# Destination stage: the first layer's two products over the mean's 48 rows stand first, one on partitions 0 to 47 and one on partitions 64 to 111

## The reference

```
x = layernorm(x + L0(x))    # [X, AX, AAX, AAAX] @ W + b, A = the weighted edges
x = layernorm(x + L1(x))    # the edge-attribute MLP, below
x = layernorm(x + L2(x))    # two-head attention over the edges
x = layernorm(x + L3(x))    # (x + 3*A'x) / 4
```

```
feat = concatenate([x, out1, out2, out3, u[batch]], axis=1)   # 128 + 48 (sum) + 48 (max) + 48 (mean) + 16
h = relu(feat @ W1 + b1)                                      # W1 has 256 columns
out = h @ W2 + b2;  return out + x
```

## Time and profile before

| | |
|---|---|
| Time, median of 3 runs | 6439.19 us (6438.15 to 6440.65) |
| Profiled execution, span | 6434.0 us |
| Instructions in the span | 102247 |
| PE busy | 4506.4 us (70%) |
| DVE busy | 4375.3 us (68%) |
| POOL busy | 4350.5 us (68%) |
| ACT busy | 3113.9 us (48%) |

### The profile page before, as it was taken

One profiled execution on the slowest core, in us unless ns is written; L12 is line 12 of the kernel. 1 busy time (PEld: TensorE's weight loads), 2 busy tenths in 40 slices (PEclk: granted clock), 3 DMA queues, 4 the chain that ended last, 5 costly groups with the idle time before them and its releaser, 6 DMA issues. The chain is left out here.

```text
span 6434.0 us, 102247 instructions
## 1 busy us (share of the span) xinstructions
PE 4506.4 (70%) x25328; PEld 3190.2 (50%) x25328; DVE 4375.3 (68%) x8181; ACT 3113.9 (48%) x6470; POOL 4350.5 (68%) x4335
## 2 busy tenths in 40 slices
PE   0059479999888799999989999978788784432200
PEld 0047367877666577777754444444444442221100
DVE  7866368888788688888853333349999996753310
ACT  0047368887666455555533333338888884110000
POOL 0057777774777577777746666647777776777777
PEclk9999789999999899999999999998888886555555
DMA  0023257777898799999955555543444435963311
GB/s 24 4 72 110 60 180 242 243 241 219 259 287 285 205 263 262 262 263 261 261 166 165 163 163 164 166 130 113 116 115 116 115 115 177 323 198 94 96 44 40
DMA packets 896637, 1090.56 MB, mean 169 GB/s; under 512 B 137109, under 2 KB 543521, under 8 KB 895492
## 3 DMA queue, kind: packets, MB, share of 16 engines
q1 hardware_dynamic: 757158, 816.08, 41.7%
q0 software_dynamic: 137984, 221.55, 13.3%
q10 hardware_dynamic: 1344, 51.38, 2.0%
HBM read 652.84 MB, written 497.99 MB: 179 GB/s over the span
## 5 line engine op out<-in xcount | busy, mean ns | idle before, releaser
L978 PE MATMUL bank<-ident,gat 128*128 128x128 f32 x2352 | 430.4, 312 | 641.8 <-DVE zT L1934 555.5
L1088 PE MATMUL bank<-W2s,hT 128*128 128x128 f32 x6272 | 779.5, 278 | 78.4 <-ACT hT L1343 78.4
L1073 PE MATMUL bank<-x1T,W1x 128*128 128x512 f32 x1568 | 776.5, 608 | 35.8 <-ACT x1T L1262 33.1
L1088 PEld LDWEIGHTS bank<-W2s,hT 128*128 128x128 f32 x6272 | 736.5, 193 | 104.9 <-ACT hT L1343 102.9
L753 POOL DMA_INDIRECT pays<-PAY,s_q x392 | 378.1, 965 | 487.9 <-DVE s_v L1800 340.0
L978 PEld LDWEIGHTS bank<-ident,gat 128*128 128x128 f32 x2352 | 297.2, 161 | 792.7 <-issue 577.0
L1272 ACT ACTIVATE mbuf<-t 128x512 f32<-128x512 f32 x490 | 310.1, 633 | 716.9 <-DVE t L1968 443.7
L978 PE MATMUL bank<-ident,x 128*128 128x128 f32 x3136 | 487.5, 279 | 195.9 <-DVE x L1901 176.7
L1343 ACT ACTIVATE hT<-bank,b1u 128x512 f32<-128x512 f32 x784 | 491.4, 677 | 248.7 <-PE bank L1076 236.3
L727 POOL DMA_INDIRECT gat<-X,d_x x392 | 392.8, 1002 | 293.9 <-issue 233.3
L1913 DVE TENSOR_TENSOR gat<-gat,pays 128x512 f32<-128x512 f32 x392 | 270.3, 689 | 451.8 <-DMA gat<-X,pays 369.0
(11 more groups left out here) (367 smaller groups left out, 11522.7 us busy)
## 6 DMA issues: line engine op xcount, KB each, us to landing
X<-x SPq DMA_DIRECT2D x588, 256.0 KB, 2.6
fB<-row_s_same SPq DMA_DIRECT2D x392, 256.0 KB
Y<-x SPq DMA_DIRECT2D x294, 256.0 KB, 3.6
xT<-in_x_fm SPq DMA_DIRECT2D x196, 256.0 KB
ffB<-rows_last_notlast SPq DMA_DIRECT2D x98, 512.0 KB
out_rows<-Y ACTq DMA_DIRECT2D x28, 1792.0 KB, 9.9
Z1T<-zT SPq DMA_DIRECT2D x98, 256.0 KB
Z1E<-zE SPq DMA_DIRECT2D x98, 256.0 KB
```

The source lines that it names most:

```text
L978: mm = pe.transpose(dst[:, t, :], tiles[t], ident[:, :])
L1073: mm = pe.matmul(bH[h][:, :, :], W1x[:, cols], x1T[s][:, :], start=True, stop=kind != "d")
L1088: mm = pe.matmul(bMLP[:, t, :], hT[h][s][:, t * P:(t + 1) * P], W2s[:, h, :], start=False, stop=h == HC - 1, skip_group_check=True)
```

## The change

In the destination stage the two W1m products stand ahead of the others. The product for the second half of the columns takes its weights and its data from partitions 64 to 111 in place of 0 to 47; for this the rows of W1 and the mean are loaded on these partitions too. The other four products follow, W1a and then W1x for each half. In other stages `chain_b2` is as it was (one W1x product for each half).

```
             for t, a in ((W1a[0:AF, :], W1[P:P + AF, :]),
                          (W1a[AM:AK, :], W1[P + AF:P + 2 * AF, :]),
-                         (W1m[0:AF, :], W1[P + 2 * AF:P + 3 * AF, :])):
+                         (W1m[0:AF, :], W1[P + 2 * AF:P + 3 * AF, :]),
+                         (W1m[AM:AK, :], W1[P + 2 * AF:P + 3 * AF, :])):
...
             def att_load(i, s):
-                if void(sp, i, s, ("ld_att", i, 32), ("ld_last", i, 16)):
+                if void(sp, i, s, ("ld_att", i, 48), ("ld_last", i, 16)):
...
-                sp.dma_start(mnt[s][0:AF, :], MNT[:, epos(g)]).then_inc(S("ld_att", s), 16)
+                for first in (0, AM):
+                    sp.dma_start(mnt[s][first:first + AF, :], MNT[:, epos(g)]).then_inc(S("ld_att", s), 16)
...
-            pe.wait_ge(S("ld_const"), 16 * 19)
+            pe.wait_ge(S("ld_const"), 16 * 20)
...
                 if kind == "d":
-                    ready(pe, "ld_att", s, i, 32)
+                    ready(pe, "ld_att", s, i, 48)
+                    for h in range(HC):
+                        rows = slice(h * AM, h * AM + AF)
+                        pe.matmul(bH[h][:, :, :], W1m[rows, h * P:(h + 1) * P], mnt[s][rows, :], start=True,
+                                  stop=False)
                 for h in range(HC):
                     cols = slice(h * P, (h + 1) * P)
-                    mm = pe.matmul(bH[h][:, :, :], W1x[:, cols], x1T[s][:, :], start=True, stop=kind != "d")
                     if kind == "d":
                         pe.matmul(bH[h][:, :, :], W1a[0:AK, cols], att[s][0:AK, :], start=False, stop=False)
-                        mm = pe.matmul(bH[h][:, :, :], W1m[0:AF, cols], mnt[s][0:AF, :], start=False, stop=True)
+                    mm = pe.matmul(bH[h][:, :, :], W1x[:, cols], x1T[s][:, :], start=kind != "d", stop=True)
                 mm.then_inc(S("hidden", s), 1)
...
-            dve.wait_ge(S("ld_const"), 16 * 19)
+            dve.wait_ge(S("ld_const"), 16 * 20)
```

## The result

The changed kernel takes 6343.8 us in the median of 4 runs (6340.8 to 6347.5) against 6439.8 us of the kernel before: a ratio of 0.9845 (95% interval 0.9833 to 0.9857), so 96 us less. It is nearest to rival B, full overlap, which was priced at 6336 us and given a chance of 0.08. A second set of runs of the same kernel on another occasion gave 6336.3 us (6329.6 to 6337.6), ratio 0.9838 (0.9824 to 0.9852).

A forecast was written before the change was run, and what follows sets the result against it. The PE and ACT loop was taken to bound the destination stage's 9.95 us step; 98 steps at -0.63 us plus 0.45 at the start gave -61.3 us, from 6439.2 to 6378 us, range 6366 to 6424.

The forecast's parts named there:

- rival B: W1m pair in the destination stage: full overlap, all records pair off, -1.06 us a step, 6336 us; chance 0.08.
- The loop of PE and ACT sets the step: Destination stage: a closed loop of PE and ACT makes the 9.95 us step; shorter first-layer products shorten it equally.
- A change of size costs 0.19 us, and one of three goes: First-layer products on PE: two changes into or out of 48 rows instead of three before the relu, -0.19 us a step.
- rival A: W1m pair: no overlap, halves run one behind the other, only the saved change of size remains, 6420 us; chance 0.21.
- I take one record, 0.43: W1m pair on PE: product two's first record starts with product one's second, so one record overlaps, 0.43 us a step.
- The bounds: Overlap of the two W1m products: gain between 0 (nothing overlaps) and 0.86 us a step (two records go).
- A change of half is free: PE between W1m products: passing from lower to upper half changes only the tile and drains nothing, no cost.
- Rival C: Between the W1m products: a change of half costs as much as a change of size, no overlap, 6440 us; chance 0.08.
- The mean's second load costs nothing in a step: SP's extra 96 KB DMA each step: 0 in the loop, +0.45 us once at the stage's start.
- POOL is late next, at 8.7 us: POOL in the destination stage: needs 8.7 us of each step, so a step of 9.32 us leaves it room.
- Rival D: PE's granted clock falls to 1.2 GHz in parts of the destination stage; 6498 us at 20 steps; chance 0.05.

The follow-up runs named there:

- e1: The changed kernel's order (W1m products first) put into the kernel before, both W1m products on partitions 0 to 47, one load of mean and weights: 6419.7 us, ratio 0.9968.
- e5: Changed kernel with each W1m product written twice, in the order lower, lower, upper, upper half: 6425.2 us in one run, 9.77 us a step.
- e2: Changed kernel with the product order of the kernel before, keeping the two halves and second loads, full-height products between the W1m products: 6440.0 us, ratio 1.0001.
- e3: Changed kernel with the W1m pair written behind the other four first-layer products instead of ahead of them: 6346.0 us, ratio 0.9853.
- e8: Changed kernel with the turning of x2 written ahead of the second-layer products and 33 VQ scatters moved to the source stage: 6311.9 us, ratio 0.9804.
- e9: Changed kernel with only the turning of x2 written ahead of the second-layer products, all VQ scatters left in the destination stage: 6336.4 us, ratio 0.9825.
- e6: e3 with 33 of the destination stage's 260 VQ scatters moved to the source stage: 6337.7 us, ratio 0.9841.
- e7: Changed kernel, W1m pair first, with only 33 VQ scatters moved to the source stage: 6353.8 us, ratio 0.9855.

## Why the prediction was wrong, by its own steps

- **The loop of PE and ACT sets the step: right.** The step fell by what the first-layer products lost, and the stage by 97 times that; the whole kernel followed.
- **A change of size costs 0.19 us, and one of three goes: right.** e1 isolates it: 0.20 us a step, 6419.7 us, where rival A had 6420.
- **"I take one record, 0.43": the step that failed.** The term is 0.86, measured 0.85 (9.75 - 8.90, e1 against the changed kernel). Its reason was that PE starts its records in their written order, so that the second product's first record could only join the first product's second. Rows 4 do show a written order, but all of their records lie on overlapping rows and could not have shown another. The runs show in its place that all records of the pair run two by two (four in 1.06 us), and e5 that a product on one half doesn't wait for one on the other half that is written before it. So the sentence ahead of the prediction, that each engine works through its instructions in their written order, doesn't hold for such products on PE. 98 x 0.42 us are 41 us; the stage's length was missed by 39 (-100.4 against -61.3), the median by 34; the other stages, whose times move from run to run, make the difference.
- **The choice between the bounds.** The bounds were 0 and 0.86, and the middle was taken on an argument that no row could bear out. The Trainium skill (TensorE: Matmul & The Clock Gate, Measured speedup vs the span model) had the right end: packed products last as long as one. Here the pair with its change of size takes 1.06 us where one product with its change took 1.05. Given 0.08, it should have been a main case, and the range should have reached it.
- **A change of half is free: right**, as the drain rule of the Trainium skill (TensorEngine Tiling (Array Packing), Key Properties) has it; the pair's second records start 0.53 behind the first, which is the one change of size and no more. Rival C falls.
- **The mean's second load costs nothing in a step: right.** e2 has the same step as before. At the stage's start it was priced at 0.45 us, one issue; the stage's start is 1.3 us longer (2.1 in e2). PE's first product now waits 4.74 us for the load where it waited 2.52, and 4.59 in e2, where a W1x product stands first: the load does this and not the order, since PE waits for all of a group's loads ahead of its first product in either kernel. The 1.3 us aren't the load's alone: e1 has one load and its first relu comes 31.7 us behind the stage's first gather, against 29.0 before, with its first products at the lower clock (four W1m records in 3.68 us).
- **POOL is late next, at 8.7 us: right, and a little low.** Where it is full (e3, e8, e9) it takes 1.32 to 1.36 us an instruction in place of 1.30 (700 us by 529, 519 and 515 instructions).
- **Rival D, the clock: fell.** The granted clock is 0.99 over the stage, and 1.00 behind its first ten us. The clock does fall in mid-stage in e3, but after waits for gathers and not from the pair.

**Open.** Whether DVE's work is what makes a VQ scatter take 1.11 us on POOL in e3 and e8 and 1.00 to 1.03 in the others. Whether the moved scatters help by POOL's time or by their DMA traffic. What moves the start of the destination stage by up to 16 us from one profile to another (3284.8 in e1, 3300.9 in the changed kernel).

## What to carry to other kernels

Two short products on different halves of the array cost as much as one, even when each float32 product is two records, and with two such products on each half they need not be written in alternation; with full-height products between them nothing is gained. Price a known mechanism that the trace can't show at its full end too, and let the range reach it; an argument from the written order of instructions is worth nothing where the rows seen could not have shown another order. When the engine that set the step gets faster, work out the next one's need for each step before going on: here the pair written last took its 0.19 us off the step only after POOL had been relieved, and the relief cost some 15 us in the source stage, so that e6 as a whole (6337.7 us) is no faster than the changed kernel.

## What the runs showed of the hardware

- Records of products on rows 0 to 47 and 64 to 111 start in pairs, 0.01 to 0.02 us apart; eight of them take 1.93 us (e5), four on the same rows 1.91 (e1).
- A product on the upper half starts ahead of a product on the lower half that is written before it (e5, inferred from the eight records in four places). The Trainium skill (TensorE: Matmul & The Clock Gate, The mechanism) has matmuls in strict order of the program at start and end; this run differs for products on different halves, and the measurement decides.
- Entering or leaving the 48-row size costs 0.19 us each time, and the place decides what it costs the kernel: behind the last product that someone waits for it is hidden, as e6 against e7 shows (8.72 against 8.90 us a step).
- In e3 the granted clock fell to 1.2 GHz five times between 3400 and 4100 us, the longest step among them after 2.48 us in which PE waited for a gather; the sixteen W2 records then took 3.62 us in place of 2.05.
